# Attention kernel with rotary embedding: the halves of the turned products swapped on TensorE instead of projected a second time

## The chip, the cores and the metric

One core of one Trainium2 chip. The metric is the device time of the whole program in microseconds (us), from runs of the same kernel; a profile of one execution stands beside it.

## The reference

The program is a small transformer block in four parts, each with a residual: attention, a mixture-of-experts feed-forward, a state-space layer, the same feed-forward again. B = 4 sequences, S = 512 tokens, D = 256. The change lies in the attention alone, with 16 heads, DH = 16 plain and DR = 64 rotary dimensions a head, and keys and values through a latent of 64:

```python
x1, x2 = jnp.split(x, 2, axis=-1)                    # _rotate_half
return jnp.concatenate([-x2, x1], axis=-1)
...
return x * cos + _rotate_half(x) * sin               # _apply_rope
...
q = (x @ Wq).reshape(Bd, Sd, H, DH + D_ROPE)
k_rope = x @ Wkr
q_rope = _apply_rope(q_rope, cos[None, :, None, :], sin[None, :, None, :])
k_rope = _apply_rope(k_rope, cos[None, :, :], sin[None, :, :])
scores = einsum(q_nope, k_nope) + einsum(q_rope, k_rope)   # scaled, causal, softmax, times v, times Wo
```

## The kernel before

The layer norm ln0 (L157 on) normalises four groups of 512 tokens, transposes them, and keeps them as a float16 high and low part, XTh and XTl. Beside it `SplitWeights` (L124 to L154) loads the attention's float32 weights and splits each block the same way: ScalarE casts the high part (L145), VectorE subtracts for the low part (L150). Blocks 0 and 1 go with group 1, blocks 2 and 3 with group 2, block 4 with group 3. A product of split operands is three float16 products (`product3`, L116 to L118), and a projection over D = 256 is six.

The rotary embedding is computed from two projections. The first, with wr, gives q of two heads in 128 rows; the second, with wt, gives the same with the halves swapped (the host has swapped the weight columns). VectorE multiplies the first by cosT and the second by sinT, whose first half is negated, into `turned` (L769 and L771). GpSimd adds the two (L836, `sum_rope`) into `rope`, ScalarE copies the high part into float16 (L684 for the key, L688 for a pair of heads), GpSimd subtracts for the low part (L848, L850), and SP's queue moves both into Q or KB.

`attention_stage` (L307 on) writes the order of each engine by hand. It goes over g = 0 to 63, one head of one sequence. For head g TensorE transposes its probabilities in float32 in three chunks (L591), computes the scores of head g+1 in three units (L579 to L581), weighs the values of head g-1 (`weigh_values`, L606 and L608), and does one "job" in two halves: the first half into bank 0 (`first_half`), the second into bank 1 (`second_half`). Even g has the job "pair" (rotary q of two heads of two cycles on), odd g the jobs oT and op of the last sequence, lat, qn, kn, kr and v of the next one, where there is one; h = 15 has none. In the order of one g TensorE does: transposes 0 and 1, scores unit 0 of g+1, first half, weigh_values(g-1), scores unit 1, transposes 2, scores unit 2, second half. VectorE does: low part of chunk 0 (L733), maxima unit 0 (L726), the second drain of the last job, low part of chunk 1, the inversion and sum of the outputs of g-1 (L742 to L745), maxima unit 1, the normalisation (L750), the first drain of this job, low part of chunk 2, maxima unit 2. ScalarE does: high part of chunk 0 (L651), exponentials of unit 2 (L644), high part of the last job's second half, high part of chunk 1, exponentials of unit 0 of g+1, high part of the first half, high part of chunk 2, `high_rope` of the last job, exponentials of unit 1 of g+1. GpSimd does the sum and low part of the last rotary job and, in even g, splits a piece of the feed-forward weights (L857, L861). SP's queue moves the pairs (L433, L438), the plain parts (L404, L416) and the keys (L423), and the weight pieces.

Ahead of the loop the list START holds the jobs ("qn", 0), ("lat", 0), ("kn", 0), ("kr", 0), ("pair", 0), ("pair", 1), ("v", 0). TensorE does both halves of one job, then of the next:

```python
for job in START:
    first_half(job)
    second_half(job)
```

## Time and profile before

| what | value |
|---|---|
| median of 3 runs | 1441.34 us (1438.83 to 1446.45) |
| the profiled execution | 1443.96 us |
| its span, first to last instruction | 1442.2 us |
| mean granted TensorE clock | 0.92 |
| TensorE matmul busy | 1169.6 us (81%) |
| VectorE busy | 985.1 us (68%) |
| ScalarE busy | 647.3 us (45%) |
| GpSimd busy | 599.3 us (42%) |

PE is TensorE's products, PEld its weight loads, DVE VectorE, ACT ScalarE, POOL GpSimd, SP the queue that issues most DMAs. A busy share is an average over stages with different limits. The matmul durations shown overlap, since products are pipelined: what a product costs is the time to the next one's start. The same holds, less so, for VectorE and ScalarE.

### The profile page before, as it was taken

To read this page: it belongs to the slowest core of one execution; us is meant where nothing else is said; L and a number is where in the kernel's file an instruction comes from. 1 tells how busy PE (TensorE), PEld (TensorE's weight loads), DVE (VectorE), ACT (ScalarE), POOL (GpSimd) and SP (SyncE) were. 2 spreads that over 40 slices of the span, in tenths; PEclk is the share of its full clock that TensorE was granted. 3 is DMA by queue.
4 is the path that set the end of the run, shared out by engine and by line. 5 is a ranking of instruction groups with operands and counts; after the bars stand their busy time and mean duration, and the time that the engine had idled before them with its cause. 6 is when DMAs were issued, how large, how long until landed. Compare 5 with 4: busy or idle time off the path is not lost. (4 is left out here: it accounts for less than half of the span.)

```text
span 1442.2 us, 32153 instructions
## 1 busy us (share of the span) xinstructions
PE 1169.6 (81%) x12288; PEld 881.9 (61%) x12288; DVE 985.1 (68%) x2082; ACT 647.3 (45%) x1519; POOL 599.3 (42%) x525
## 2 busy tenths in 40 slices
PE   2789898998874599998817885998999648999992
PEld 1356566665653398987713553665766527989882
DVE  6479798887786556456565956788797574555554
ACT  4367566666564133333446653353333223333342
POOL 0245445545430234334300195688696213333220
PEclk9899999999995599999958998999999759999996
DMA  4655756656533598876240002000000039966635
GB/s 158 155 131 157 175 167 172 167 164 158 147 111 87 197 419 345 277 248 252 66 173 8 15 25 45 16 17 2 2 2 2 27 93 397 419 238 243 253 99 186
DMA packets 98186, 216.83 MB, mean 150 GB/s; under 512 B 28977, under 2 KB 68146, under 8 KB 91890
## 3 DMA queue, kind: packets, MB, share of 16 engines
q1 hardware_dynamic: 88434, 192.22, 41.0%
q0 software_dynamic: 7488, 20.46, 4.2%
q8 instruction: 99, 1.62, 0.5%
q10 hardware_dynamic: 2112, 2.10, 0.4%
q14 instruction: 53, 0.43, 0.1%
HBM read 157.40 MB, written 40.04 MB: 137 GB/s over the span
## 5 line engine op out<-in xcount | busy, mean ns | idle before, releaser
L1228 ACT ACTIVATE ffn_h<-ffn_bank,ffn_b 128x256 f32<-128x256 f32 (+1 forms) x384 | 143.9, 431 | 278.5 <-PE ffn_bank L118 259.3
L1407 DVE CAST ffn_hh<-ffn_h 128x512 f16<-128x512 f32 (+1 forms) x192 | 80.7, 420 | 182.8 <-ACT ffn_h L1228 166.5
L116 PE MATMUL ffn_bank<-ffn_hh,ffn_W 128*128 128x256 f16 (+1 forms) x768 | 181.0, 254 | 8.9 <-DVE ffn_hl L1409 8.9
L1042 POOL DMA_INDIRECT ffn_xs<-xn_rows,ffn_from_rows x78 | 79.4, 1019 | 244.4 <-PE ffn_bank L1123 158.2
L118 PE MATMUL ffn_bank<-ffn_hh,ffn_W 128*128 128x256 f16 (+1 forms) x768 | 180.8, 254 | 0.0
L117 PE MATMUL ffn_bank<-ffn_hl,ffn_W 128*128 128x256 f16 (+1 forms) x768 | 180.7, 253 | 0.0
L644 ACT ACTIVATE att_prob<-att_bank,att_nmax 128x512 f32<-128x512 f32 (+3 forms) x256 | 127.1, 525 | 31.3 <-DVE att_nmax L726 30.0
L733 DVE TENSOR_TENSOR att_ptl<-att_bank,att_pth 128x384 f16<-128x384 f32 (+1 forms) x192 | 113.9, 593 | 34.4 <-ACT att_pth L651 34.4
L651 ACT ACTIVATE att_pth<-att_bank 128x384 f16<-128x384 f32 (+1 forms) x192 | 101.3, 528 | 79.0 <-PE att_bank L591 79.0
L1049 POOL DMA_INDIRECT y_rows<-ffn_y,ffn_to_rows x78 | 77.4, 993 | 133.6 <-DVE ffn_y L1418 86.9
L591 PE MATMUL att_bank<-main_identf,att_prob 128*128 128x128 f32 x640 | 99.6, 281 | 35.7 <-ACT att_prob L644 19.6
L2344 POOL TENSOR_TENSOR ssm_L<-ssm_L,ssml_G 128x512 f32<-128x512 f32 x86 | 110.8, 1302 | 39.5 <-DVE ssm_L L2251 39.4
L2175 ACT ACTIVATE ssmh_windows<-ssml_dtx 64x64 f32<-64x64 f32 x256 | 64.7, 253 | 138.4 <-PE ssm_Y L2074 132.4
L836 POOL TENSOR_TENSOR att_rope<-att_turned 128x512 f32<-128x512 f32 x36 | 45.6, 1267 | 192.3 <-DVE att_turned L771 138.2
L726 DVE TENSOR_REDUCE att_nmax<-att_bank 128x1 f32<-128x512 f32 (+3 forms) x256 | 117.6, 479 | 10.7 <-PE att_bank L581 10.3
L1409 DVE TENSOR_TENSOR ffn_hl<-ffn_h,ffn_hh 128x512 f16<-128x512 f32 (+1 forms) x192 | 115.6, 602 | 6.6
L591 PEld LDWEIGHTS att_bank<-main_identf,att_prob 128*128 128x128 f32 x640 | 71.9, 143 | 56.5 <-ACT att_prob L644 42.6
L2251 DVE TENSOR_TENSOR_SCAN ssm_L<-ssm_bank,ssmh_ident 128x512 f32<-128x512 f32 x86 | 102.1, 1207 | 5.4 <-PE ssm_bank L2062 4.9
L116 PE MATMUL ffn_bank<-ffn_xTh,ffn_W 128*128 128x256 f16 (+1 forms) x384 | 92.1, 257 | 3.4 <-DVE ffn_xTl L1400 3.4
L116 PE MATMUL ffn_bank<-ffn_W,ffn_hh 128*128 128x256 f16 x312 | 85.3, 273 | 9.3 <-DVE ffn_hl L1409 8.8
L117 PE MATMUL ffn_bank<-ffn_xTl,ffn_W 128*128 128x256 f16 (+1 forms) x384 | 92.2, 257 | 0.0
L118 PE MATMUL ffn_bank<-ffn_xTh,ffn_W 128*128 128x256 f16 (+1 forms) x384 | 92.0, 256 | 0.0
(345 smaller groups left out, 3222.6 us busy)
## 6 DMA issues: line engine op xcount, KB each, us to landing
ffn_W<-split_w SPq DMA_DIRECT2D x46, 2048.0 KB, 19.3
att_piece<-in_ffn_w SPq DMA_DIRECT2D x32, 512.0 KB, 5.2
split_w<-att_halves SPq DMA_DIRECT2D x32, 512.0 KB, 4.2
att_Q<-att_pair SPq DMA_DIRECT2D x64, 128.0 KB, 2.4
ffn_back<-y_rows SPq DMA_DIRECT2D x16, 512.0 KB, 9.1
att_KB<-att_krl SPq DMA_DIRECT2D x8, 512.0 KB, 5.6
att_Q<-att_pair SPq DMA_DIRECT2D x64, 64.0 KB, 2.1
xn_rows<-ffn_XN SPq DMA_DIRECT2D x8, 512.0 KB, 2.6
```

What stands on the lines that cost most here:

```text
L116: pe.matmul(out, ah, bh, start=start, stop=False)
L117: pe.matmul(out, ah, bl, start=False, stop=False)
L118: return pe.matmul(out, al, bh, start=False, stop=stop)
L591: ins = pe.transpose(bk[:, j * P:(j + 1) * P], prob[:, g % 2, at + j * P:at + (j + 1) * P], identf[:, :])
L644: ins = act.activation(prob[:, g % 2, p_at[i]:p_at[i] + n], bank[bk][:, at:at + n], ACT.Exp, bias=nmax[:, g % 2, i:i + 1])
L651: act.activation(pth[:, g % 2, at:at + n], bank[5 + (3 * g + c) % 2][:, 0:n], ACT.Copy).then_inc(pT_high, 1)
L726: ins = dve.tensor_reduce(nmax[:, g % 2, i:i + 1], bank[bk][:, at:at + (i + 1) * P], AX.X, ALU.max, negate=True)
L733: dve.tensor_tensor(ptl[:, g % 2, at:at + n], bank[5 + (3 * g + c) % 2][:, 0:n], pth[:, g % 2, at:at + n], ALU.subtract).then_inc(pT_low, 1)
L1228: ins_ = act.activation(h[layer][:, m, 0:n], bank[1 + 2 * layer + u][:, (m % 2) * n:(m % 2 + 1) * n], ACT.Gelu, bias=bias[:, ds(e + m, 1)])
L1409: dve.tensor_tensor(hl[layer][:, half, 0:n], h[layer][:, half, 0:n], hh[layer][:, half, 0:n], ALU.subtract).then_inc(h_low[layer], 1)
L2251: dve.tensor_tensor_scan(slots[p % RING], bank[p % 2][:, :], ident8[:, :], 0.0, ALU.mult, ALU.add).then_inc(scan_done, 1)
L2344: pool.tensor_tensor(slots[p % RING], slots[p % RING], G[:, b, :], ALU.mult).then_inc(mult_done, 1)
```

## The change

The second projection is gone, and with it the swapped weights wt, their DMA and their split. VectorE multiplies the one projection in bank 0 by both tables, cosine and sine, one after the other, in the place of the first drain. TensorE's second half of a pair or kr job is `turn_half`: a float32 product of a signed permutation `swap` with the sine part and a float32 product of the identity with the cosine part, summed in bank 1. It waits for both of VectorE's products. ScalarE reads bank 1 twice, for the float16 high part and for a float32 copy `rope`, in the place where the second halves of other jobs are read; GpSimd no longer adds and only subtracts for the low part. In START the first half of the next job now stands ahead of the second half of this one. VectorE makes `swap` from the identity with two small instructions. The diff, cut to its core (declarations, unpacking and the shapes of wx are left out):

```diff
@@ tensor @@
+            def turn_half(job):
+
+                at = turn[job] % 2
+                pe.wait_ge(swap_made, 2)
+                pe.wait_ge(first_drained, nth[job] + 1)
+                pe.matmul(bank[1][:, :], swap[:, :], turned[:, at, 1, :], start=True, stop=False)
+                return pe.matmul(bank[1][:, :], identf[:, :], turned[:, at, 0, :], start=False, stop=True)
...
-                if what == "pair":
-                    ins = project(bank[1][:, :], wth, wtl, n % (NH // 2) * P, P, n // (NH // 2))
-                elif what == "kr":
-                    ins = project(bank[1][:, :], wxh, wxl, KT_AT, P, n)
+                if what in ("pair", "kr"):
+                    ins = turn_half(job)
...
-            for job in START:
-                first_half(job)
+            first_half(START[0])
+            for job, following in zip(START, START[1:] + [None]):
+                first_half(following)
                 second_half(job)
@@ scalar @@
+                if what in ("pair", "kr"):
+                    if x:
+                        high_rope(job)
+                    return
...
                 r = turn[job]
-                act.wait_ge(summed, r + 1)
+                act.wait_ge(second_ready, nth_second[job] + 1)
                 if what == "kr":
-                    ins = act.activation(KA[:, n % 2, :], rope[:, r % 2, :], ACT.Copy)
+                    ins = act.activation(KA[:, n % 2, :], bank[1][:, :], ACT.Copy)
                 else:
                     if n >= 2:
                         act.wait_ge(moved[n % 2], moved_by(n - 2))
-                    ins = act.activation(pair[:, n % 2, 0, :], rope[:, r % 2, :], ACT.Copy)
+                    ins = act.activation(pair[:, n % 2, 0, :], bank[1][:, :], ACT.Copy)
                 ins.then_inc(rope_high, 1)
+                if r >= 2:
+                    act.wait_ge(rope_low, r - 1)
+                act.activation(rope[:, r % 2, :], bank[1][:, :], ACT.Copy).then_inc(second_drained, 1)
...
-                if last:
-                    high_rope(last)
@@ vector @@
+            halves_of = lambda a: a[:, :].rearrange("p (b x r) -> p b x r", x=2, r=HALF)
+            for x in range(2):
+                dve.tensor_scalar(halves_of(swap)[:, :, x, :], halves_of(identf)[:, :, 1 - x, :], -1.0, None, ALU.mult).then_inc(swap_made, 1)
...
-                if what == "lat" and x:
+                if what in ("lat", "pair", "kr") and x:
                     return
...
-                    r, table = turn[job], sinT if x else cosT
+                    r = turn[job]
                     if r >= 2:
-                        dve.wait_ge(summed, r - 1)
-                    to = turned[:, r % 2, x, :]
-                    if what == "kr":
-                        ins = dve.scalar_tensor_tensor(to, bank[x][:, :], ATT_SCALE, table[:, :], ALU.mult, ALU.mult)
-                    else:
-                        ins = dve.tensor_tensor(to, bank[x][:, :], table[:, :], ALU.mult)
+                        dve.wait_ge(second_ready, nth_second[ropes[r - 2]] + 1)
+                    for at, table in enumerate((cosT, sinT)):
+                        to = turned[:, r % 2, at, :]
+                        if what == "kr":
+                            ins = dve.scalar_tensor_tensor(to, bank[0][:, :], ATT_SCALE, table[:, :], ALU.mult, ALU.mult)
+                        else:
+                            ins = dve.tensor_tensor(to, bank[0][:, :], table[:, :], ALU.mult)
@@ gpsimd @@
-                pool.tensor_tensor(rope[:, r % 2, :], turned[:, r % 2, 0, :], turned[:, r % 2, 1, :], ALU.add).then_inc(summed, 1)
...
                 wait_alone(pool, rope_high, r + 1, passed)
+                wait_alone(pool, second_drained, nth_second[job] + 1, passed)
@@ weights @@
-            (rows(ins["att_turned"][0]), *wr), (rows(ins["att_turned"][1]), *wt), (rows(ins["att_mixed"]), *wx),
+            (rows(ins["att_rope"]), *wr), (rows(ins["att_mixed"]), *wx),
...
-    mixed = np.concatenate([nope, Wdkv, Wkr, Wkr, swap(Wkr), swap(Wkr)], axis=1)
+    mixed = np.concatenate([nope, Wdkv, Wkr, Wkr], axis=1)
```

## Rows read from the trace of the kernel before

**Rows 1.** Busy time by stage: stretch, length, engines' busy us (instructions), PEclk, DMA.
```profile
11.20:35.14 23.94, 7.76 (x32) 6.28 (x33) 21.64 (x61) 17.87 (x30) 0.00 (x0) 1.00 0.38 129
35.14:65.40 30.26, 20.61 (x84) 8.73 (x84) 10.69 (x18) 7.83 (x13) 8.19 (x7) 0.88 0.58 134
65.40:440.00 374.60, 330.88 (x3304) 227.82 (x3303) 312.15 (x804) 238.41 (x509) 178.44 (x129) 0.95 0.57 153
```

**Rows 2.** Waits within 70 to 420 us: who for whom, total us, times, longest.
```profile
POOL att_rope L836 <- DVE att_turned L771: 138.2, 27, 7.8
...
PE att_bank L591 <- ACT att_prob L644: 17.9, 12, 1.9
PE att_bank L591 <- DVE att_ptl L733: 14.5, 17, 1.6
```

**Rows 3.** Timeline of TensorE, g = 24: start, duration, what; idle before in brackets.
```profile
208.47 0.32 PE L579 MATMUL att_bank<-att_KA,att_Q 128*128 128x384 f16 x1
...
209.64 0.38 PE L116 MATMUL att_bank<-attw_XTh,attw_wth 128*128 128x512 f16 x1
...
210.93 0.27 PE L591 MATMUL att_bank<-main_identf,att_prob 128*128 128x128 f32 x1
```

**Rows 4.** Timeline of VectorE in the same head.
```profile
208.89 0.17 DVE L742 RECIPROCAL att_rinv<-att_bank 128x4 f32<-128x4 f32 x1
...
209.94 0.68 DVE L771 TENSOR_TENSOR att_turned<-att_bank,attw_cosT 128x512 f32<-128x512 f32 x1
210.54 0.54 DVE L733 TENSOR_TENSOR att_ptl<-att_bank,att_pth 128x384 f16<-128x384 f32 x1
```

**Rows 5.** Timeline of TensorE in the state-space layer, float32 products.
```profile
862.44 1.88 PE L1690 MATMUL proj_bank<-proj_starts,main_identf 128*128 128x512 f32 x4
864.16 0.38 PE L116 MATMUL proj_bank<-ssmi_XTh,ssmi_wih 128*128 128x512 f16 x1
```

**Rows 6.** Timelines of ScalarE, TensorE, VectorE, an odd head without job and the next.
```profile
400.18 0.50 ACT L651 ACTIVATE att_pth<-att_bank 128x384 f16<-128x384 f32 x1
...
403.17 0.63 ACT L688 ACTIVATE att_pair<-att_rope 128x512 f16<-128x512 f32 x1 [1.07 <-POOL att_rope L836]
403.71 0.56 ACT L644 ACTIVATE att_prob<-att_bank,att_nmax 128x384 f32<-128x384 f32 x1
...
402.20 0.63 PE L591 MATMUL att_bank<-main_identf,att_prob 128*128 128x128 f32 x4 [0.67 <-DVE att_ptl L733]
404.32 0.55 PE L591 MATMUL att_bank<-main_identf,att_prob 128*128 128x128 f32 x3 [1.49 <-ACT att_prob L644]
404.71 0.38 PE L579 MATMUL att_bank<-att_KA,att_Q 128*128 128x512 f16 x1
...
401.51 0.55 DVE L733 TENSOR_TENSOR att_ptl<-att_bank,att_pth 128x384 f16<-128x384 f32 x1
```

**Rows 7.** Busy time of three even heads, columns as in the first group.
```profile
377.24:386.00 8.76, 7.27 (x55) 4.37 (x56) 6.07 (x18) 4.24 (x9) 5.17 (x4) 0.81 0.35 101
402.15:409.46 7.31, 5.76 (x54) 3.76 (x55) 6.04 (x17) 4.24 (x9) 5.25 (x4) 1.00 0.24 56
205.35:210.93 5.58, 5.58 (x55) 3.70 (x54) 5.13 (x14) 4.05 (x9) 4.28 (x3) 1.00 0.56 159
```

**Rows 8.** One line's instructions: ns min/median/max, first and last start.
```profile
L750 DVE TENSOR_TENSOR att_O<-att_both,att_rinv x64: 213/319/1106, 76.4 to 432.6; 128x64 f32<-128x64 f32 x64
```

**Rows 9.** The removed block's split on ScalarE and VectorE, columns as before.
```profile
L145 ACT ACTIVATE attw_wth<-ln_staged x1: 1908/1908/1908, 23.2 to 23.2; 128x2048 f16<-128x2048 f32 x1
...
L150 DVE TENSOR_TENSOR attw_wtl<-ln_staged,attw_wth x1: 2283/2283/2283, 25.5 to 25.5; 128x2048 f16<-128x2048 f32 x1
```

**Rows 10.** Timelines of the start of attention, VectorE and SP's queue.
```profile
47.41 0.69 DVE L769 SCALAR_TENSOR_TENSOR att_turned<-att_bank,attw_cosT 128x512 f32<-128x512 f32 x1 [0.91 <-PE att_bank L118]
...
52.94 0.70 SPq L423 DMA_DIRECT2D att_KB<-att_krl  x1
53.69 3.41 SPq L416 DMA_DIRECT2D att_KB<-nope  x3
```

More of the change, by code:

```diff
@@ L307, in attention_stage @@
 def attention_stage(nc, X, XTh, XTl, weights, identf, identb, upper_neg, cosT, sinT, ffn_w, split_w, nope, xn_rows):
-    (wrh, wrl), (wth, wtl), (wxh, wxl), (wuh, wul), (woh, wol) = weights
-    QN_AT, LAT_AT, KR_AT, KT_AT = 0, NH * DH, NH * DH + LAT, NH * DH + LAT + P
+    (wrh, wrl), (wxh, wxl), (wuh, wul), (woh, wol) = weights
+    QN_AT, LAT_AT, KR_AT = 0, NH * DH, NH * DH + LAT
     NG, NPR = B * NH, B * NH // 2
@@ L318, in attention_stage @@
         turned, rope = t.sb("turned", [P, 2, 2, S]), t.sb("rope", [P, 2, S])
-        pair = t.sb("pair", [P, 2, 2, S], F16)
+        pair, swap = t.sb("pair", [P, 2, 2, S], F16), t.sb("swap", [P, P])
         qnh, qnl, knh, knl = (t.sb(n, [P, 2, S], F16) for n in ("qnh", "qnl", "knh", "knl"))
@@ L336, in attention_stage @@
         first_drained, second_drained = sem("first_drained"), sem("second_drained")
-        summed, rope_high, rope_low = sem("summed"), sem("rope_high"), sem("rope_low")
+        swap_made, rope_high, rope_low = sem("swap_made"), sem("rope_high"), sem("rope_low")
         moved = [sem(f"moved{i}") for i in range(2)]
@@ L367, in attention_stage @@
         nth_second = {job: n for n, job in enumerate(j for j in done if j[0] != "lat")}
-        turn = {job: n for n, job in enumerate(j for j in done if j[0] in ("pair", "kr"))}
+        ropes = [j for j in done if j[0] in ("pair", "kr")]
+        turn = {job: n for n, job in enumerate(ropes)}
         def wait_drained(eng, job):
@@ L678, in high_rope @@
                 what, n = job
-                if what not in ("pair", "kr"):
-                    return
                 r = turn[job]
-                act.wait_ge(summed, r + 1)
+                act.wait_ge(second_ready, nth_second[job] + 1)
                 if what == "kr":
-                    ins = act.activation(KA[:, n % 2, :], rope[:, r % 2, :], ACT.Copy)
+                    ins = act.activation(KA[:, n % 2, :], bank[1][:, :], ACT.Copy)
                 else:
@@ L693, in _ @@
                 high_half(job, 1)
-                high_rope(job)
             probs(0, 0)
@@ L826, in _ @@
         def _(pool):
-            def sum_rope(job):
-                what, n = job
-                if what not in ("pair", "kr"):
-                    return
-                r = turn[job]
-                wait_alone(pool, first_drained, nth[job] + 1, passed)
-                wait_alone(pool, second_drained, nth_second[job] + 1, passed)
-                if r >= 2:
-                    wait_alone(pool, rope_high, r - 1, passed)
-                pool.tensor_tensor(rope[:, r % 2, :], turned[:, r % 2, 0, :], turned[:, r % 2, 1, :], ALU.add).then_inc(summed, 1)
             def low_rope(job):
@@ L864, in _ @@
             for job in START:
-                sum_rope(job)
                 low_rope(job)
@@ L869, in _ @@
                 if last:
-                    sum_rope(last)
                     low_rope(last)
@@ L2404, in attention_layer @@
         XTh, XTl = pair("XT", [P, KD, B * S])
-        wr, wt, wx = pair("wr", [P, KD, NH * DR]), pair("wt", [P, KD, NH * DR]), pair("wx", [P, KD, NH * DH + LAT + 4 * DR])
+        wr, wx = pair("wr", [P, KD, NH * DR]), pair("wx", [P, KD, NH * DH + LAT + 2 * DR])
         wu, wo = pair("wu", [LAT, NH * 2 * DH]), pair("wo", [P, KD, D])
@@ L2408, in attention_layer @@
         parts = [
-            (rows(ins["att_turned"][0]), *wr), (rows(ins["att_turned"][1]), *wt), (rows(ins["att_mixed"]), *wx),
+            (rows(ins["att_rope"]), *wr), (rows(ins["att_mixed"]), *wx),
             (ins["att_up"], *wu), (rows(ins["L0_attn_a_Wo"]), *wo)]
         layer_norm_stage(nc, "ln0", X, XTh, XTl, c["identf"], lambda t: SplitWeights(t, parts))
-        attention_stage(nc, X, XTh, XTl, (wr, wt, wx, wu, wo), c["identf"], identb, upper_neg, cosT, sinT, ffn_w,
+        attention_stage(nc, X, XTh, XTl, (wr, wx, wu, wo), c["identf"], identb, upper_neg, cosT, sinT, ffn_w,
                         split_w, nope, xn_rows)
@@ L2451, in attention_weights @@
     rope, nope = q[:, :, DH:], q[:, :, :DH].reshape(D, NH * DH)
-    swap = lambda w: np.concatenate([w[..., HALF:], w[..., :HALF]], axis=-1)
-    turned = np.stack([rope.reshape(D, NH * DR), swap(rope).reshape(D, NH * DR)])
-    mixed = np.concatenate([nope, Wdkv, Wkr, Wkr, swap(Wkr), swap(Wkr)], axis=1)
+    mixed = np.concatenate([nope, Wdkv, Wkr, Wkr], axis=1)
     up = Wukv.reshape(LAT, NH, 2, DH).transpose(0, 2, 1, 3).reshape(LAT, 2 * NH * DH)
-    return {"att_turned": turned, "att_mixed": mixed, "att_up": up}
+    return {"att_rope": rope.reshape(D, NH * DR), "att_mixed": mixed, "att_up": up}
 def ssm_weights(W_in, conv_w, conv_b, D, norm_w, W_out, mup_vector):
```

## The prediction

> **What bounds the kernel now.** The profiled execution took 1443.96 us (span 1442.2); the runs' median is 1441.34, so I sum against 1443.96 and take 2.6 off at the end. By stage [rows 1], the change touches three stretches: the first layer norm with the weight split (11.2 to 35.1), the start of attention (35.1 to 65.4), and its loop of 64 heads (65.4 to 440). In the loop TensorE is busy 330.9 of 374.6 us, VectorE 312.2, ScalarE 238.4, GpSimd 178.4. So GpSimd, which loses work, is the engine with the most room, and the question is what TensorE and VectorE do.
>
> Next the waits of the loop [rows 2]. GpSimd waits 138 us for the turned tile: its sum is off the path nearly always. TensorE waits 17.9 us (12 times) for ScalarE's exponentials and 14.5 us for VectorE, and little else.
>
> Then one pair of heads in order of time. Only even g holds a rotary "pair" job. In g = 24, where the odd heads beside it have jobs too, TensorE issues without a gap: weigh_values is over at 208.47, the second projection starts at 209.64, is six products, and the transposes of the next head start at 210.93, so it is worth 1.29 us, 0.215 a product [rows 3]. The window of this head shows TensorE busy 5.58 of 5.58 us [rows 7]. VectorE in the same stretch runs one instruction after the other: the inversion of the sums at 208.89, the cosine product at 209.94, the next instruction at 210.54 [rows 4]. It reaches the cosine product 0.30 us after TensorE began the second projection. Today this costs nothing, because nobody on TensorE waits for it soon. That is the row on which the forecast rests.
>
> **The change, part by part.**
>
> (1) TensorE's second half. Six float16 products go (1.29 us), two float32 products 128x512 come. The trace of before has such products: four records take from 862.44 to the next product at 864.16, 0.43 us a record [rows 5], and the loop at L1690 issues two products there, so a float32 product is two records, 0.86 us. Two make 1.72 us: +0.43 us a job, on 36 jobs (32 pairs, 4 kr), 33 of them in the loop (30 and 3).
>
> (2) The new wait. turn_half waits for both VectorE products of its own job (first_drained is raised by the sine product). In the kernel before the second projection waited only for its bank. VectorE's place for the pair does not move: the cosine product at 209.94, then 0.60 us to the next start [rows 4], then the sine product of 0.68 us, and 0.14 us until TensorE starts (VectorE's piece of 0.55 us from 401.51 ends at 402.06 and TensorE goes on at 402.20 [rows 6]). The turned tile is there at 209.94 + 0.60 + 0.68 + 0.14 = 211.36; TensorE arrives at 209.64. It stands 1.72 us. Queued behind it on TensorE are the transposes of the next head, and all engines follow those, so the stall is on the path. Both sides hang on the same event, the end of weigh_values: VectorE's inversion needs it, and TensorE has only the scores and one group of transposes (1.17 us) between it and the turn. So the stall should recur alike in every even g. With (1): 1.72 + 0.43 = 2.15 us a job. The sine product that left odd g gives nothing back there, since TensorE had no gap in it. Bounds: 0.43 if VectorE could be early, 2.5 where it is later (a kr job in an odd head, where ScalarE's copies of the last pair sit ahead of the piece that VectorE waits for). Taken: 33 x 2.15 = 71.0 us.
>
> (3) ScalarE and GpSimd. The sum of 1.27 us goes from GpSimd, hidden but for ScalarE: in heads without other jobs the copy of the pair waits 1.07 us for GpSimd, at 403.17, and the exponential behind it starts at 403.71, for which TensorE waits 1.49 us until 404.32 [rows 6]. After the change ScalarE reads the bank twice (about 0.5 us each from start to start, as its other copies) right after 400.18 instead, waiting for nobody, because the turn ends before the next transposes start. This puts some 1.05 us before the high part that starts at 400.18 today; VectorE's piece behind it, at 401.51 today because the sine product stood before it, comes about 0.2 us later. It frees the later exponential by about 0.5 us. TensorE's wait of 1.49 then ends with VectorE's low part, about 0.3 us earlier. 12 waits x 0.3 = -3.6 us. Bounds: 0 to -17.9 (all of that wait [rows 2]). GpSimd's low part waits for ScalarE's second copy, half a microsecond; its user, the DMA to Q, is due three heads later: nothing.
>
> GpSimd's freed time has one more road. VectorE's L750, a small operation with operands in SBUF, takes 213 ns at best, 319 in the median, 1106 at worst [rows 8]; the long ones lie beside GpSimd's instructions. The Trainium skill (SBUF — State Buffer, "SBUF: two separate sides") says that VectorE with two SBUF inputs and GpSimd exclude each other for a whole instruction; the trace agrees. By that rule the change would return up to 0.1 us a head, 64 x 0.1 = 6 us at most, and this rule speaks for the change; I leave it in the range, since GpSimd's other instructions stay.
>
> (4) The weight split. One block of 2048 columns goes: 1.91 us on ScalarE and 2.28 on VectorE [rows 9], both in back-to-back work of their engines; the mixed block shrinks from 1152 to 896 columns (some 0.2 us). One DMA of 1024 KB goes, which nobody waited for. VectorE is the longer: -2.4 us, between 0 and -3.
>
> (5) The start. The order is now first half of the next job, then second half of this one. The next first half needs bank 0 drained, and no second product fills that wait. Up to the kr job this puts the second halves of qn and kn, with their drains, ahead of the drains of lat and kr on VectorE: about 2.5 us. From kr's cosine product to the issue of get_keys it is 47.41 to 52.94 = 5.5 us now [rows 10]; after: two VectorE products 1.3, the next pair's projection 1.3, the turn 1.7, two copies 1.1, the subtraction 1.15 and handovers of 0.1 to 0.2 us, some 7.0. So 1.5 more. get_keys is the head of SP's queue, with 3.4 us of key DMAs and then the pair's behind it; the first scores follow those. So +4 us, and more if TensorE, idle oftener, runs this at half clock: up to +10. Taken +5.
>
> (6) The clock. In two heads with the same work and the same 1.49 us wait, one takes 8.76 us at a granted clock of 0.81, the other 7.31 at 1.00 [rows 7]: a fall to 1.2 GHz follows some waits of TensorE and costs some 1.45 us. The loop's 0.95 over 374.6 us [rows 1] means some 37 us at half clock now. The new stalls, 33 of 1.7 us, are about as long as the waits of these two heads, of which one brought a fall and one did not. I take four more: +6 us; bounds 0 and 30 more (+43).
>
> Sum: 71.0 - 3.6 - 2.4 + 5 + 6 = +76.0; 1443.96 + 76.0 = 1520.0, on the scale of the median 1517.
>
> **The rivals.**
> Clock: TensorE falls to 1.2 GHz after nearly every stall. For it: [rows 7]; against it: the second head there, whose wait of 1.49 us left the clock at 1.00. 1517 + 26 x 1.45 = 1555. The Trainium skill (TensorE: Matmul & The Clock Gate, "HAM oscillation — how this bites in real kernels") describes a kernel whose TensorE waits once in each tile and is throttled again in each; it would speak for this one.
> Hidden wait: VectorE runs ahead, because a sine product left the odd heads, and the turn finds its tile ready. Then only (1) is paid: 33 x 0.43 = 14.2, with 5 - 2.4: 1461 - 2.6 = 1458. Against it: VectorE starts from weigh_values' end, not from its backlog [rows 3, 4].
> float32 at the transposes' rate: those are float32 too, and three of 128 columns take 0.39 us from 404.32 to 404.71 [rows 6], 0.13 each, so some 0.5 for 512 columns. If the product cost one record of 0.43, (1) would be -0.43: 1517 - 33 x 0.86 = 1489. Against it: [rows 5].
> The other side: TensorE's whole wait for exponentials in the loop falls away (-17.9), VectorE's L750 returns 6, the split 2.4, the stall is hidden; with +14.2 of (1) and no loss at the start 1441.3 - 12.1 = 1429, faster. It decides if VectorE delivers the sine product within 0.3 us of today's cosine start, or if the waits of [rows 2] all hang on GpSimd's sum.
> The change not doing what it says would be a turn that doesn't wait; the wait is there for each job.
>
> **How the numbers follow.** Forecast, stall in each job, 0.66, own range 1495 to 1540. Clock 0.12, float32 rate 0.06, hidden wait 0.11, other side 0.05. The range reaches over the slow cases but for the hidden wait and the far end of the clock: 1482 to 1555. About 0.5% (7 us) is what a measurement of this kernel can tell from no change: faster 0.04, same 0.05, slower 0.91.
>
> **What would show it.** In each even head TensorE should have a gap of 1.7 us before the first record of the turn, ended by the turned tile, and four float32 records spaced 0.43. ScalarE should wait for nobody before the pair's copy. The loop should be some 70 to 80 us longer, the layer norm 2.4 shorter, the start 4 to 10 longer. Wrong it is if the gap is under 1 us, if the granted clock of the loop falls below 0.9, or if VectorE is no longer gapless between the inversion and the pair's products.

## The result and the profile after

| | before | after |
|---|---|---|
| median | 1442.08 us (1438.83 to 1446.45, 4 runs) | 1525.07 us (1524.83 to 1525.70, 4 runs) |
| span of the profiled execution | 1442.2 us | 1523.3 us |

The change makes the kernel slower: 1.0574 times the time before, 95% interval 1.0545 to 1.0603. 1517 was forecast, with 1482 to 1555 as the range.

The busy time by stage answers to [rows 1]: the split of the weights, the start of attention, the loop up to the last head's transposes (columns: stretch, length, busy of PE, PEld, DVE, ACT, POOL with instructions, granted clock, DMA share, GB/s).

```profile
11.40:33.40 22.00, 7.76 (x33) 6.31 (x34) 19.41 (x60) 15.98 (x29) 0.00 (x0) 1.00 0.27 87
33.40:72.50 39.10, 25.95 (x78) 9.52 (x78) 10.65 (x20) 9.21 (x16) 4.68 (x5) 0.76 0.44 104
72.50:504.10 431.60, 342.84 (x3162) 226.96 (x3160) 314.62 (x785) 247.18 (x534) 136.55 (x96) 0.97 0.50 133
```

In the kernel before, the transposes of the last head start at 426.5. The stretch to compare is this one:

```profile
65.40:426.50 361.10, 322.27 (x3228) 221.26 (x3226) 305.22 (x785) 234.21 (x501) 178.44 (x129) 0.96 0.59 159
```

So the span's 81.1 us are: loop 431.6 - 361.1 = +70.5; start 39.1 - 30.3 = +8.8; everything up to attention's first product 33.4 - 35.1 = -1.7; everything behind the loop +3.5. TensorE's busy time in the loop rose by 20.6 us only, so 50 us of the 70 are time in which it stands (88.8 us for 38.8). GpSimd does 42 us less in the loop, and nothing that these rows show comes of it.

TensorE in the same head, g = 24, as in [rows 3]:

```profile
242.18 0.22 PE L588 MATMUL att_bank<-attw_upper_neg,attw_identb 128*128 128x128 bf16 x1
243.74 1.10 PE L514 MATMUL att_bank<-att_turned,att_swap 128*128 128x512 f32 x2 [1.34 <-DVE att_turned L785]
244.67 1.02 PE L515 MATMUL att_bank<-att_turned,main_identf 128*128 128x512 f32 x2
245.53 0.71 PE L598 MATMUL att_bank<-main_identf,att_prob 128*128 128x128 f32 x5
```

The last product of the scores issues at 242.18, and products of its size follow each other by 0.06 us here, so the turn could have started at 242.24 and starts at 243.74: 1.50 us later. The view shows this as 1.34 us idle, since the duration that it gives a product runs past the place of the next. The turn itself takes 243.74 to 245.53 = 1.79 us where the second projection took 1.29. VectorE beside it, as in [rows 4]:

```profile
241.25 0.18 DVE L755 RECIPROCAL att_rinv<-att_bank 128x4 f32<-128x4 f32 x1
...
242.31 0.68 DVE L785 TENSOR_TENSOR att_turned<-att_bank,attw_cosT 128x512 f32<-128x512 f32 x1
242.92 0.68 DVE L785 TENSOR_TENSOR att_turned<-att_bank,attw_sinT 128x512 f32<-128x512 f32 x1
243.51 0.55 DVE L746 TENSOR_TENSOR att_ptl<-att_bank,att_pth 128x384 f16<-128x384 f32 x1
```

The sine product ends at 243.60, TensorE goes on 0.14 us later. Over the loop TensorE's waits are these (who for whom, total us, times, longest); 33 of them, 48.5 us, are the new one (1.34 us in most heads, as in g = 24, and up to 2.4):

```profile
PE att_bank L514 <- DVE att_turned L785: 43.1, 30, 2.4
PE att_bank L598 <- DVE att_ptl L746: 40.0, 37, 2.4
PE att_bank L514 <- DVE att_turned L783: 5.4, 3, 1.8
```

In [rows 2] the transposes waited 17.9 us for exponentials and 14.5 for VectorE's low part. The first has gone from the list and the second has grown to 40.0.

### The profile page after: what moved, and what is told of

It is laid out like the page before. It is cut to its first block and busy times, and to the rows that moved or that the text cites. A ratio compares the mean times of both kernels' runs of the same rounds, so it can differ in the third digit from the quotient of the medians.

```text
span 1523.3 us, 31940 instructions
## 1 busy us (share of the span) xinstructions
PE 1198.1 (79%) x12216; PEld 889.9 (58%) x12216; DVE 993.1 (65%) x2083; ACT 660.3 (43%) x1554; POOL 553.1 (36%) x489
## 5 line engine op out<-in xcount | busy, mean ns | idle before, releaser
L854 POOL TENSOR_TENSOR att_pair<-att_rope,att_pair 128x512 f16<-128x512 f32 x32 | 37.1, 1159 | 262.7 <-ACT att_rope L702 262.7
L598 PE MATMUL att_bank<-main_identf,att_prob 128*128 128x128 f32 x640 | 100.0, 281 | 41.1 <-DVE att_ptl L746 40.0
```

Of the source, the lines that this page charges most:

```text
L598: ins = pe.transpose(bk[:, j * P:(j + 1) * P], prob[:, g % 2, at + j * P:at + (j + 1) * P], identf[:, :])
```

## The experiments

The times of the stages in each trace, read as above: start of attention is from its first product to the first transposes of the loop, the loop from there to the last head's transposes. "Behind" is the rest of the span after attention's last product, and the code there is the same in all.

The runs were taken on four chips, and the kernel before was run beside them on each: 1441.02 us beside wait_only, one_product, late_turn and late_reads; 1436.52 (13 runs, 1431.46 to 1443.44) beside early_drain, old_start, second_later and copy_after_exp; 1443.36 (11 runs, 1439.40 to 1447.27) beside early_old_start, idle_drain_later and idle_drain_before; 1435.78 beside new_start_before. The stretch behind goes with this: 1003.6 to 1005.0 us, 997.0 to 999.5, 1003.4 to 1004.0 and 996.6 in these four groups. So a difference between two totals of different groups holds some 5 us that no edit made, and the totals of kernels with a single run are good to a few us only. The stages are the better measure, and a total is best compared as its distance to the run of the kernel before beside it, which is +83.0 for the changed kernel.

| kernel | time, us | start | loop | behind |
|---|---|---|---|---|
| before | 1442 | 30.3 | 361.1 | 1001.2 |
| after | 1525 | 39.1 | 431.6 | 1004.6 |
| wait_only | 1474 | 31.5 | 387.1 | 1004.4 |
| one_product | 1505 | 38.8 | 410.6 | 1005.0 |
| late_turn | 1512 | 41.1 | 417.1 | 1003.6 |
| late_reads | 1518 | 39.9 | 424.3 | 1004.0 |
| early_drain | 1476 | 38.9 | 387.8 | 999.4 |
| old_start | 1511 | 29.5 | 432.3 | 999.5 |
| early_old_start | 1473 | 31.4 | 388.9 | 1004.0 |
| second_later | 1472 | 33.6 | 390.4 | 998.7 |
| idle_drain_later | 1462 | 33.9 | 374.4 | 1004.0 |
| new_start_before | 1448 | 40.3 | 359.0 | 996.6 |
| copy_after_exp | 1434 | 29.7 | 355.9 | 997.0 |
| idle_drain_before | 1438 | 29.6 | 354.8 | 1003.4 |

**The wait by itself** (wait_only, on the kernel before):

```diff
+                if what in ("pair", "kr"):
+                    pe.wait_ge(first_drained, nth[job] + 1)
                 if what == "pair":
                     ins = project(bank[1][:, :], wth, wtl, ...)
```

> The kernel before, with nothing of the change but the wait: the second projection of a pair or kr job waits until VectorE's cosine product of the same job is done. My theory (TensorE stands because VectorE's place for the pair comes after the inversion): the cosine product ends at 209.94 + 0.68, plus 0.14, against 209.64, so 1.12 us a job, 33 jobs, +37 us, 1478 us; a gap of about 1.1 us before line L116 of the second projection in each even head. Rival (the wait is hidden, the change's loss is the float32 products and the clock): within 5 us of 1442. Rival (handing over costs more than the gap, as the clock falls after each): over 1500.

It took 1474.29 us beside 1441.02, +33, and the loop +26.0. TensorE in g = 24:

```profile
221.34 0.38 PE L116 MATMUL att_bank<-attw_XTh,attw_wth 128*128 128x512 f16 x1 [0.96 <-DVE att_turned L773]
```

That is 0.96 us of idle time, 1.12 with the 0.16 by which the duration shown for the product ahead runs on, as worked out. A wait on one VectorE product costs the 1.12 us in a head where TensorE had no gap, and nothing else of the change is needed for it. Over the loop the new wait is 30.2 us (33 times), and the loop grew by 26.0 where 37 were expected: in part the new wait takes the place of others that were there. VectorE's sine product still stands in the odd heads here, so this run does not test the hidden wait of the prediction; the 33 gaps in the changed kernel itself disprove that one.

**One of the two float32 products** (one_product; it leaves out the cosine part of the rotary q and k):

```diff
-                pe.matmul(bank[1][:, :], swap[:, :], turned[:, at, 1, :], start=True, stop=False)
-                return pe.matmul(bank[1][:, :], identf[:, :], turned[:, at, 0, :], start=False, stop=True)
+                return pe.matmul(bank[1][:, :], swap[:, :], turned[:, at, 1, :], start=True, stop=True)
```

> The changed kernel with one of the two float32 products of the turn left out (the identity's, so the cosine part is missing from the rotary q and k). If the turn lies wholly on the path, 0.86 us goes for each of the 33 jobs of the loop: -28 us, and some 2 us at the start, 1495 us. If TensorE's products are hidden behind VectorE or ScalarE in part of the heads (the heads without other jobs), -15 to -20 us. Rival (float32 products don't matter, only the wait does): within 5 us of 1525. The gap before the turn stays at 1.3 to 1.5 us in every theory of mine.

1504.52 us, -20.6, loop -21.0. In g = 24:

```profile
237.97 1.10 PE L514 MATMUL att_bank<-att_turned,att_swap 128*128 128x512 f32 x2 [1.35 <-DVE att_turned L784]
238.91 0.60 PE L597 MATMUL att_bank<-main_identf,att_prob 128*128 128x128 f32 x4
```

The gap is the same and the turn takes 0.94 us for 1.79: one product less is 0.85 us in each even head. 33 of these would be 28 us; the loop gave 21. The granted clock of the loop fell beside it, from 0.97 over 431.6 us to 0.95 over 410.7, which is about 26 and 41 us at 1.2 GHz as these rounded values have it:

```profile
72.00:482.70 410.70, 324.12 (x3097) 219.05 (x3095) 315.89 (x785) 246.88 (x534) 136.78 (x97) 0.95 0.52 140
```

15 us more at half clock cost up to 7.5, which is about the size of the missing part. That is arithmetic on two rows, not an experiment on the clock; the granted clock over the whole span goes from 0.911 to 0.927 in repeated runs of the kernel before, so one trace each does not show that the edit lowered it.

**The turn in the next head** (late_turn): second half of a pair or kr job after the next head's first half, ahead of weigh_values, and the two reads of ScalarE where the old copy stood.

```diff
                 first_half(job)
+                if g >= 1 and rotary(job_at(g - 1)):
+                    second_half(job_at(g - 1))
                 if g >= 1:
                     weigh_values(g - 1)
...
-                second_half(job)
+                if not rotary(job):
+                    second_half(job)
```

> The changed kernel with the turn put into the next head, after its first half and ahead of weigh_values, and ScalarE's two reads of the bank back where the copies stood before. The work is the same, and the turned tile has been ready for 3 us by then. My theory: the gap before the turn goes (33 x about 1.9 us, 62 us, with the delay of the chain), the float32 products stay (+14), the slower start stays (+8.9): 1460 to 1475 us. Rival (the gap is lost capacity of VectorE and comes back at the next wait): 1500 or more. Rival (ScalarE's reads, now late, hold the exponentials that TensorE needs): 1480 to 1500, with more waiting of the transposes for ScalarE.

1511.97 us, loop -14.5: my first theory, that moving the turn away from its gap would return it, fell here. The gap before the turn is gone, but TensorE stands almost as long as in the changed kernel, 417.10 - 332.31 = 84.8 us for 88.8; the rest of the 14.5 is busy time, at a granted clock of 0.99 where it was 0.97:

```profile
74.30:491.40 417.10, 332.31 (x3161) 221.13 (x3160) 303.19 (x785) 249.57 (x534) 136.88 (x96) 0.99 0.52 138
```

VectorE in the odd head (ready for the inversion at 245.7):

```profile
245.19 0.55 DVE L752 TENSOR_TENSOR att_ptl<-att_bank,att_pth 128x384 f16<-128x384 f32 x1
247.74 0.18 DVE L761 RECIPROCAL att_rinv<-att_bank 128x4 f32<-128x4 f32 x1 [2.00 <-PE att_bank L617]
```

The turn holds weigh_values back, VectorE stands 2.00 us for it, in order, with the maxima of the next head's unit 1 behind, and TensorE pays at the next transposes (52.8 us in 34 waits for VectorE's low part, 14.3 in 13 for exponentials). It also waits 17.7 us in 15 for ScalarE's reads of bank 1, which this edit made late. "DVE att_rinv <- PE" is 71.0 us in 44 waits in that loop; in the changed kernel the same wait is 8.9 us in 11 waits. My reading is that a head is one chain, values, inversion, maxima, exponentials, transposes, and that work put ahead of it on TensorE comes back as a wait in it.

**ScalarE's reads in their old place** (late_reads): the call of high_rope again behind the high part of chunk 2, the rest of the changed kernel unchanged.

> The changed kernel with only ScalarE's two reads of bank 1 moved back to where high_rope stood (after the high part of chunk 2). It tells what the early reads cost or give. In even heads the turn starts 4.74 us after the first transposes where the old second half started 4.29 us after them, 0.45 us that my prediction put at 0.2. If the early reads are the cause (they hold the high part of chunk 1 and VectorE behind it), this gives 0.45 us in about 20 heads back, -9 us, 1516; in the heads without other jobs the two late reads hold an exponential and cost 0.5 us, 9 to 12 heads, +5, so 1515 to 1522. If GpSimd's collisions with VectorE are the cause: no change or slower, 1525 to 1535.

1518.15 us, loop -7.3. In g = 24 the head falls from 8.03 to 7.80 us, not by the 0.45 expected, but the head behind it takes 6.00 us where it takes 4.63 in the changed kernel, since its second half now has to wait until ScalarE has read bank 1:

```profile
247.20:253.20 6.00, 4.68 (x49) 2.87 (x47) 4.37 (x12) 4.61 (x10) 0.65 (x1) 1.00 0.16 63
252.52 0.37 PE L116 MATMUL att_bank<-att_ckh,attw_wuh 64*128 64x512 f16 x1 [1.32 <-ACT att_rope L700]
```

Over the loop TensorE's waits change hands. The low part of VectorE holds the transposes 1.6 us in one wait (40.0 in the changed kernel), exponentials 17.5 us in 23 waits, and ScalarE's late reads hold the next product into bank 1 20.0 us in 15 waits. In all TensorE stands 424.30 - 335.68 = 88.6 us, as in the changed kernel (88.8):

```profile
73.20:497.50 424.30, 335.68 (x3161) 225.22 (x3160) 300.81 (x785) 246.78 (x534) 136.89 (x97) 0.99 0.51 135
```

The 7.3 us are busy time of TensorE, at a granted clock of 0.99 where it was 0.97. So the place of the reads moves waits from one to the other, and what the early reads cost or gain is nothing that this run shows. That the time fell into the expected range says nothing for the theory behind it, which had no price for the head behind.

**VectorE's products ahead of the inversion** (early_drain):

```diff
                 low_probs(g, 1)
+                if job and job[0] in ("pair", "kr"):
+                    drain(job, 0)
                 if g >= 1:
                     invert_sums(g - 1)
...
-                if job:
+                if job and job[0] not in ("pair", "kr"):
                     drain(job, 0)
```

> The changed kernel, but VectorE makes a pair's two products (and kr's) right after the low part of chunk 1, ahead of the inversion and maxima of unit 1. The theory that the gap before the turn is set by VectorE's place for the pair: the products then start about 1.0 us earlier than after the inversion, sum, maxima and normalisation, so the gap falls from 1.34 us to some 0.3 to 0.5; but the inversion and the maxima of unit 1 come 1.2 us later, and the exponentials and the transposes of the next head with them. If TensorE's gap alone counts: -1.0 x 33, 1492. If, as the late turn suggests, each head is a chain that takes back what is moved (weights of values, inversion, maxima, exponentials, transposes): 1510 to 1530, with the wait now before the next head's transposes.

1475.56 us, -49.5, or -44.0 when each is taken from the kernel before beside it (+39.0 for +83.0), and loop -43.8: more than the 33 I gave the gap alone, and the rival, by which the chain takes back what is moved, is out. VectorE in g = 24, and TensorE:

```profile
223.07 0.68 DVE L785 TENSOR_TENSOR att_turned<-att_bank,attw_cosT 128x512 f32<-128x512 f32 x1
223.67 0.68 DVE L785 TENSOR_TENSOR att_turned<-att_bank,attw_sinT 128x512 f32<-128x512 f32 x1
224.26 0.17 DVE L755 RECIPROCAL att_rinv<-att_bank 128x4 f32<-128x4 f32 x1
...
224.49 1.10 PE L514 MATMUL att_bank<-att_turned,att_swap 128*128 128x512 f32 x2 [0.19 <-DVE att_turned L785]
```

The same instructions, on the same engines; only their order on VectorE changed. The gap falls to 0.19 us here and to 7.5 us in 21 waits over the loop (48.5 before this mend), and VectorE's wait for weigh_values, 8.9 us in 11 waits in the changed kernel, is gone. The delayed inversion cost little: the transposes' wait for VectorE's low part is 41.5 us, it was 40.0.

**The order of the start** (old_start, the changed kernel with the old loop over START; new_start_before, the kernel before with the new one):

```diff
-            first_half(START[0])
-            for job, following in zip(START, START[1:] + [None]):
-                first_half(following)
-                second_half(job)
+            for job in START:
+                first_half(job)
+                second_half(job)
```

> The changed kernel with the order of the start as before (both halves of a job, then the next job), the turns left as they are. In the changed kernel the first transposes of the loop start 39.1 us after the attention's first product, before it was 30.2: +8.9. If the new order is the cause (TensorE idles for the drain of bank 0, qn's and kn's second halves stand ahead of lat and kr, and it falls to half clock): 5 to 7 us come back, 1518 to 1520, although the turns of kr and two pairs now have no cover (some 3 us each). If the turns themselves are the cause, no change or slower: 1525 to 1532.

> The kernel before with the changed kernel's order of the start and nothing else: the first half of the next job ahead of the second half of this one, the second half of kr and the pairs still a float16 projection. If the order alone makes the slower start (39.1 against 30.3 us in the changed kernel, 29.5 with the old order put back): the time from the attention's first product to the loop's first transposes rises by 5 to 9 us, to 35 to 39, and the kernel with it. If it needs the turns, which wait for their own job's products: under 3 us, 33 or less.

old_start: 1510.77 us (-14.3, or -8.7 when each is taken from the kernel before beside it; 5 to 7 were expected), its start 29.5 for 39.1. new_start_before: 1447.63 beside 1435.78, its start 40.3 for 30.3. Undone and done alone, the order is worth 9.6 and 10.0 us, and the turns cost nothing that shows. The first products of TensorE in new_start_before that had to wait show why: each is a first half and waits for VectorE to drain bank 0, with nothing in between.

```profile
39.49 0.64 PE L116 MATMUL att_bank<-attw_XTh,attw_wxh 128*64 128x512 f16 x1 [1.41 <-DVE att_qnl L781]
45.88 0.58 PE L116 MATMUL att_bank<-att_ckh,attw_wuh 64*128 64x512 f16 x1 [2.09 <-DVE att_ckl L778]
48.73 0.61 PE L116 MATMUL att_bank<-attw_XTh,attw_wxh 128*128 128x512 f16 x1 [1.42 <-DVE att_knl L784]
54.87 0.39 PE L116 MATMUL att_bank<-attw_XTh,attw_wrh 128*128 128x512 f16 x1 [2.01 <-DVE att_turned L770]
```

The second of them needs what VectorE writes there as its operand, and waits in the kernel before too, for 1.49 us. Up to the loop TensorE's waits for a drain are 10.7 us in seven in new_start_before and 2.3 in two in the kernel before. TensorE's busy time in the start rises beside them from 20.61 [rows 1] to 25.11 us, at a granted clock of 0.80 for 0.88, and the wait for the pair's DMA ahead of the first scores falls from 7.25 to 4.53.

**Both mends together** (early_old_start).

> The changed kernel with both single mends: the start in the old order and VectorE's two products ahead of the inversion. The runs of each alone gave -49.5 and -14.3 us against 1525. If the two causes are independent: 1525 - 64 = 1461, within 5 us. If the earlier products change what bounds the start: off by more than 5.

1473.44 us, 12 more than 1461, and so by my own measure not independent. But the numbers that I added come from different chips. Taken from the kernel before beside each, the mends alone are at +39.0 and +74.3 where the changed kernel is at +83.0, so the two should be at +30.3, and they are at +30.1. The stages say the same: start 31.4 (29.5 alone) and loop 388.9 (387.8). With one run each, this is good to a few us.

**Every second half one head later** (second_later): second_half(job_at(g - 1)) at the end of head g, read and drained one head later as well, a third pair made in the start, and the start in the old order.

> The changed kernel with every second half of a job one head later, at the same place of the head (and read and drained one head later), and the pairs made three ahead instead of two, the third in the start; the start in the old order. The turn then finds its tile ready, and nothing is put ahead of weigh_values. If the loss of the change is the missing cover of the turn and not its work: the gap before the turn is under 0.1 us, the heads with all jobs fall from 12.7 a pair to about 11.9 (11.1 + 0.43 + some waiting of the next transposes for VectorE's low part), 1455 to 1480. If VectorE's and ScalarE's added work in the even head is the limit, the time goes into waits of the transposes and stays over 1500.

1472.12 us, loop 390.4. No gap stands before the turn any more and nothing is ahead of weigh_values, but the transposes wait 49.1 us in 33 waits for VectorE's low part:

```profile
224.74 0.52 PE L599 MATMUL att_bank<-main_identf,att_prob 128*128 128x128 f32 x3 [0.92 <-DVE att_ptl L747]
...
228.12 1.07 PE L515 MATMUL att_bank<-att_turned,att_swap 128*128 128x512 f32 x2
229.03 1.02 PE L516 MATMUL att_bank<-att_turned,main_identf 128*128 128x512 f32 x2
229.89 0.27 PE L599 MATMUL att_bank<-main_identf,att_prob 128*128 128x128 f32 x1
```

VectorE ahead of the first of these lines:

```profile
222.86 0.68 DVE L786 TENSOR_TENSOR att_turned<-att_bank,attw_cosT 128x512 f32<-128x512 f32 x1
223.46 0.67 DVE L786 TENSOR_TENSOR att_turned<-att_bank,attw_sinT 128x512 f32<-128x512 f32 x1
224.06 0.54 DVE L747 TENSOR_TENSOR att_ptl<-att_bank,att_pth 128x384 f16<-128x384 f32 x1
```

So 29.3 of the loop's 70.5 us are left without any wait of the turn. The two VectorE products stand ahead of the low part of chunk 2, and the next run tells what that place is worth.

**The products where VectorE idles** (idle_drain_later, second_later with this; idle_drain_before, the kernel before with it and with copy_after_exp):

```diff
+                if last and last[0] in ("pair", "kr"):
+                    drain(last, 0)
                 low_probs(g, 0)
...
-                if job:
+                if job and job[0] not in ("pair", "kr"):
                     drain(job, 0)
```

> The changed kernel with the second halves one head later (as in the run second_later) and with VectorE's two products of a pair or kr job at the start of the next head. In second_later the transposes waited 47.9 us (32 times) for VectorE's low part, because both products stood ahead of it. My theory that the change's own work costs TensorE 0.43 us a job and all the rest of its 70 us is the place of VectorE's products: those waits fall under 20 us, the loop to 365 to 375 us (361.1 before), 1440 to 1455 in all with the third pair in the start. If VectorE's drains can't be hidden (bank 0 freed too late for the next first half): 1460 or more.

1461.92 us, ratio to before 1.0133 (1.0096 to 1.0170); loop 374.4, as forecast, 16.0 less than in second_later; the waits for the low part 20.1 us in 23. The total was forecast 7 us too low, and it is past the 1460 of the rival, that bank 0 is freed too late. That rival is there, and small: first halves wait for VectorE's two products 9.9 us in 18 waits, one of them in the head behind g = 24:

```profile
219.86 0.37 PE L116 MATMUL att_bank<-att_ckh,attw_wuh 64*128 64x512 f16 x1 [0.63 <-DVE att_turned L786]
```

The loop stays 13.3 us over the kernel before:

```profile
67.20:441.60 374.40, 333.66 (x3150) 224.15 (x3150) 309.23 (x783) 248.85 (x532) 134.63 (x95) 0.97 0.56 152
```

TensorE is busy 11.4 us longer than before and stands 40.7 us where it stood 38.8. 33 x 0.43 = 14.2 would be the price of the float32 products alone. That fits, but not because all else stayed: the waits for bank 0 came, and those for exponentials fell from 17.9 us [rows 2] to 1.6.

**ScalarE's copy behind the exponentials** (copy_after_exp, on the kernel before): ScalarE's high_rope stands behind probs(g + 1, 1) instead of ahead of it.

> The kernel before with one thing of the change alone, in another way: ScalarE no longer waits for GpSimd's sum ahead of the exponentials of unit 1; its copy of the pair stands behind them. My part (3) put the gain of this at 0.3 us in each of the 12 waits of TensorE for exponentials, -3.6 us, with -17.9 as the far bound: 1436 to 1440. If all those waits hang on GpSimd's sum: 1425. If it moves them to VectorE's low part or delays the pair's DMA: 1441 to 1446.

Ratio 0.9973 (0.9952 to 0.9994), 1433.74 us beside 1436.52: a gain of 0.3%, which the interval only just tells from none; it holds the -3.6 us of the forecast's part (3), and the 17.9 us of the rival called the other side are out. The exponentials are gone from TensorE's waits in the loop but for 1.1 us (17.9 in [rows 2]), and VectorE's low part took over (29.9 us in 38 waits, 14.5 in [rows 2]); the loop is 5.2 us shorter.

And the same with VectorE's cosine product moved too (idle_drain_before):

> The kernel before with ScalarE's copy of the pair behind the exponentials (as in the last run) and with VectorE's cosine product of a pair or kr job at the start of the next head, where VectorE waits for ScalarE's first high part. The theory that the loop of before is held by VectorE's low part of chunk 2, for which the next head's transposes wait (38 waits, 29.9 us in the run with the copy moved): the cosine product no longer stands ahead of it, 0.6 us in each such head, so 8 to 18 us less, 1416 to 1428. If TensorE's own work is the bound in most heads: within 5 us of 1434. If bank 0, drained 1 us later, holds the next first half: 1440 or more.

Ratio 0.9961 (0.9940 to 0.9983), 1438.01 us beside 1443.36. Its loop is 354.8 against 355.9 with the copy alone, and its interval covers that one's ratio: the second edit brought nothing that can be told apart. The forecast of 8 to 18 us was wrong: the transposes still wait 26.0 us in 30 waits for VectorE's low part. Why moving the product freed so little of this was not tested. In a head with jobs on both sides, as g = 24, which stays at 5.6 us, TensorE's own work is the bound.

## Why the prediction was right, point by point

**The step that carried it.** VectorE reaches the pair too late for a turn in the same head: predicted a gap of 1.72 us, and 33 gaps were there, 1.50 us in g = 24 and 48.5 us in all as the view counts them. wait_only shows the gap from one added wait, early_drain shows that VectorE's order sets it. The handover of 0.14 us came out exactly and the 0.60 from start to start as 0.61.

**The float32 products.** Predicted 1.72 us for two, +0.43 a job; measured 1.79 and +0.50 in g = 24; one left out gave 0.85 there. Each of the two is two records, so the rival at the transposes' rate is out.

**A job.** Predicted 2.15 us. In g = 24 the head grew from 5.58 [rows 7] to 8.03:

```profile
237.50:245.53 8.03, 6.36 (x53) 3.87 (x52) 7.03 (x18) 3.74 (x8) 1.94 (x1) 1.00 0.55 170
```

which is 2.45 = 1.50 + 0.50 + 0.45. The term I missed is the last one: the turn's arrival moved from 4.29 to 4.74 us after the head's first transposes, because the second group of transposes waits for VectorE's low part of the head before:

```profile
237.73 0.54 DVE L746 TENSOR_TENSOR att_ptl<-att_bank,att_pth 128x384 f16<-128x384 f32 x1
...
238.42 0.52 PE L598 MATMUL att_bank<-main_identf,att_prob 128*128 128x128 f32 x3 [0.32 <-DVE att_ptl L746]
```

I had this delay, 0.2 us for ScalarE's early reads, but held it against VectorE only and not against the next transposes. Seen from VectorE, the turned tile was ready 6.24 us after the head's first transposes where the prediction had 6.01 (211.36 - 205.35), so the gap was smaller than forecast only because TensorE was late too. Heads without other jobs grew less: 9.00 us, where 7.31 stood in [rows 7]. Over all 33 jobs the loop's 70.5 us are 2.14 a job, beside the 2.15 forecast; that this fits so well is luck, since it averages heads of 2.45 and of 1.69.

**ScalarE and GpSimd.** The wait for exponentials went, as said, and ScalarE waits for nobody ahead of the pair's copy in the loop. In a head without other jobs the wait of 1.49 us ended as forecast, with VectorE's low part and 0.2 us earlier, but the delay of 0.2 us that I had put on VectorE's piece came back in the wait ahead of it, 0.86 us where [rows 6] have 0.67:

```profile
408.99 0.63 PE L598 MATMUL att_bank<-main_identf,att_prob 128*128 128x128 f32 x4 [0.86 <-DVE att_ptl L746]
410.88 0.52 PE L598 MATMUL att_bank<-main_identf,att_prob 128*128 128x128 f32 x3 [1.26 <-DVE att_ptl L746]
```

So the -3.6 us did not come, and the wait for the low part rose from 14.5 to 40.0 us in all. GpSimd's 42 us less are worth nothing that shows. The median of VectorE's small operation of [rows 8] fell to 224 ns, nearer its 213, and its longest rose to 1940; the loop doesn't tell of it.

```profile
L763 DVE TENSOR_TENSOR att_O<-att_both,att_rinv x64: 213/224/1940, 84.9 to 510.2; 128x64 f32<-128x64 f32 x64
```

One of the long ones, 0.59 us at 236.62, lies beside GpSimd's cast from 236.09 to 237.13: the exclusion moved, it did not end.

**The weight split.** -2.4 predicted. From the first layer norm instruction to attention's first product it is 33.40 - 11.51 against 35.17 - 11.26 = -2.0.

**The start.** +5 predicted, with 10 as the bound, +8.8 measured. The mechanism was right and its size was off, by the clock: I took the end of the range at full clock, and the granted clock of this stretch is 0.76 where it was 0.88 [rows 1]. From attention's first product to kr's cosine product it is 16.73 us, 12.24 before (50.13 - 33.40 and 47.41 - 35.17): +4.5, for 2.5 forecast. From there to SP's get_keys it is 9.98 us, 5.5 before and 7.0 forecast:

```profile
50.13 0.68 DVE L783 SCALAR_TENSOR_TENSOR att_turned<-att_bank,attw_cosT 128x512 f32<-128x512 f32 x1
51.46 0.61 PE L116 MATMUL att_bank<-attw_XTh,attw_wrh 128*128 128x512 f16 x1 [2.61 <-DVE att_turned L783]
...
53.99 1.92 PE L514 MATMUL att_bank<-att_turned,att_swap 128*128 128x512 f32 x2
...
57.58 0.60 ACT L694 ACTIVATE att_KA<-att_bank 128x512 f16<-128x512 f32 x1 [8.09 <-PE att_bank L515]
...
60.11 0.70 SPq L424 DMA_DIRECT2D att_KB<-att_krl  x1
```

The pair's projection takes 2.53 us here and the turn some 3.5, where 1.3 and 1.7 were put: the 3.0 us more are these two at half clock (granted clock 0.52 from 51.46 to 57.58).

**The clock.** +6 predicted; wrong in sign. The loop's granted clock is 0.97, it was 0.96 over the same loop of before: six falls to 1.2 GHz in the loop, for seven before, although 33 gaps came. One of two like heads fell again, 10.50 us at 0.84 against 9.00 at 1.00:

```profile
409.00:418.00 9.00, 6.40 (x53) 3.91 (x54) 7.28 (x20) 4.04 (x9) 3.31 (x3) 1.00 0.80 198
462.00:472.50 10.50, 7.90 (x53) 4.54 (x54) 7.28 (x20) 4.04 (x9) 3.31 (x3) 0.84 0.45 134
```

The Trainium skill (TensorE: Matmul & The Clock Gate, "HAM oscillation — how this bites in real kernels") tells of a kernel that falls at every wait between tiles. Its waits are of some 3 to 5 us by the page, longer than the 1.2 to 2.4 us of the turn here, so the trace neither bears the page out nor speaks against it, and the page was weak support for the clock rival of the prediction.

**Not in the sum.** 3.5 us behind the loop, in code that didn't change. The traces of these runs differ by up to 8 us there, and mostly from one chip to the other, so I don't count it as the change's.

In all the loop's 70.5 us were forecast as 73.4, the start's 8.8 as 5, and the 3.5 behind not at all. The sum of +76 is 7 us short of the measured +83.0, and it is that near partly by luck: the clock's +6, which did not come, stands in for the 4 that the start's term lacked.

## What to carry to other kernels

When an engine's work is made dependent on another engine's result in the same round, read from the trace where in its hand-written order that other engine makes it, and count from the event that starts both; if the producer's place is late, move the producer before giving up the change (here two VectorE products moved ahead of the inversion were worth 44 us of loop without any instruction less). Work taken off the engine with the most room was worth nothing that showed here (42 us of GpSimd), and moving a gap away by putting work ahead of the chain's next link only moved it (late_turn, late_reads). When a wait is gone from the list, add up how long the bound engine stands in all: in late_reads it stood exactly as long as before. In a start sequence with one bank for the first halves, the second half of each job covers the drain of that bank; interleaving the jobs took this cover away and cost 10 us.

## What the runs showed of the hardware that I had not expected

A float32 product 128x512 by a 128x128 float32 matrix takes 0.86 us of TensorE (244.67 to 245.53), four times a float16 product (0.215 us), while three float32 transposes of 128 columns take 0.39 us [rows 6]. The first product of a turn, the one by the permutation, takes 0.93 us behind a wait (243.74 to 244.67) and 0.91 in second_later, where nothing waits (228.12 to 229.03), so the 0.05 to 0.07 us more are not the wait's; whether they are the permutation's or the first place's was not tested. The granted clock of the loop did not fall below that of before for 33 waits of 1.2 to 2.4 us. In the one trace in which a product of 0.85 us was taken out behind each of them it was lower (0.95), and in those of late_turn and late_reads, where TensorE stands as long, higher (0.99). The same code behind attention took 996.6 to 999.5 us on two of the chips and 1003.4 to 1005.0 on the other two.
